# First and second mixture: tokens listed by expert, 39 gathered tiles of 128 in place of eight dense experts

## The reference, cut to what matters

```python
x = x + tanh(g_xattn[0]) * attention0(ctx, layernorm(x))
# layer 0: xf = layernorm(x), 2048 x 128
spk = (xf @ Wg.T + bg > 1.0)                     # 2048 x 8
topv, topi = top_k(spk, 2);  topw = softmax(topv)
for e in range(8):
    h = silu(xf @ w1[e].T + b1[e]) * (xf @ w3[e].T + b3[e])   # 512 wide
    y = (h > 1.0) @ w2[e].T + b2[e]
    out += comb[:, e] * y                        # comb: topw at topi, zero elsewhere
x = x + tanh(g_ffn[0]) * out
# layer 1: attention, then a ternary feed-forward part (silu, gelu, gelu)
# layer 2: attention, then
idx, scores = top_k(xf @ Wg + bg, 2) with softmax
h = gelu(xf @ W1[e] + b1[e]);  y = h @ W2[e] + b2[e]
out = layernorm(xf + sum over the two of score * y) * gamma + beta
x = x + tanh(g_ffn[2]) * out
# layer 3: attention, then a mixture of eight small experts (not touched)
```

## Time and profile before

| | us |
|---|---|
| median of three runs | 1279.51 |
| lowest, highest | 1269.94, 1280.77 |
| profiled execution, whole | 1281.16 |
| its span (first to last instruction) | 1279.8 |

### The profile page before, as it was taken

The page is one execution under the profiler, slowest core; times in us unless marked ns, Lnnn a source line. Parts: engine busy times, 40 slices in busy tenths (PEclk is TensorE's granted clock), DMA queues, the critical chain, the costliest instruction groups (busy, mean ns, idle before and its releaser), DMA issues.

```text
span 1279.8 us, 22233 instructions
## 1 busy us (share of the span) xinstructions
PE 1075.3 (84%) x8405; PEld 822.7 (64%) x8405; DVE 795.9 (62%) x1613; ACT 514.1 (40%) x846; POOL 314.7 (25%) x545
## 2 busy tenths in 40 slices
PE   3677799999999679997777899899954888888888
PEld 2455677777777556766566677677742667767655
DVE  3677568788887863333245367999983456652555
ACT  0344544333333223322134377667720245554412
POOL 5233111232221222224334012332234112200200
PEclk9978999999999589998589789999985599996999
DMA  4300001321210200000100012313000000000162
GB/s 145 115 11 11 7 26 30 100 74 63 92 33 1 91 0 1 1 1 34 54 20 23 10 34 68 92 50 91 34 0 9 18 15 15 16 16 2 38 207 94
DMA packets 35176, 55.70 MB, mean 44 GB/s; under 512 B 4192, under 2 KB 18048, under 8 KB 34816
## 3 DMA queue, kind: packets, MB, share of 16 engines
q1 hardware_dynamic: 34640, 53.11, 13.7%
q10 hardware_dynamic: 432, 1.18, 0.2%
HBM read 47.26 MB, written 1.25 MB: 38 GB/s over the span
## 4 chain that ended last, share of the span: by engine, by line
PE 59%; DVE 20%; issue 6%; ACT 5%; DMA 4%; POOL 4%; SPq 1%; POOLq 0%; DVEq 0%; ACTq 0%
PE banks L386 9%; PE banks L159 8%; PE banks L161 8%; PE banks L160 8%; DVE NM L456 4%; PE banks L394 4%; PE bank L407 4%; PE bank L1604 2%; PE bank L1407 2%; PE bank L159 2%; DMA QT<-NMT 2%; DVE TT L1391 2%; PE bank L161 2%; PE bank L160 2%; ACT EE L430 2%
## 5 line engine op out<-in xcount | busy, mean ns | idle before, releaser
L456 DVE TENSOR_REDUCE NM<-banks 128x4 f32<-128x1024 f32 (+1 forms) x112 | 136.9, 1222 | 159.8 <-PE banks L386 159.8
L386 PE MATMUL banks<-KT,QT 31*128 31x128 f32 (+1 forms) x1280 | 163.1, 391 | 73.7 <-DMA QT<-NMT 25.1
L386 PEld LDWEIGHTS banks<-KT,QT 31*128 31x128 f32 x1280 | 114.9, 227 | 107.0 <-issue 37.0
L430 ACT ACTIVATE EE<-banks 128x1024 f32<-128x1024 f32 x112 | 114.6, 1024 | 166.9 <-PE banks L394 166.8
L394 PE MATMUL banks<-QT,KT 32*128 32x128 f32 x1792 | 155.9, 317 | 4.7 <-ACT EE L430 3.5
L1384 ACT ACTIVATE SG<-banks,VC 128x512 f32<-128x512 f32 x128 | 88.2, 689 | 151.0 <-PE banks L161 150.9
L394 PEld LDWEIGHTS banks<-QT,KT 32*128 32x128 f32 x1792 | 129.0, 214 | 8.9 <-issue 6.6
L1391 DVE SCALAR_TENSOR_TENSOR TT<-banks,VC,SG 128x512 f32<-128x512 f32 x128 | 95.9, 749 | 48.8 <-ACT SG L1384 45.8
L1444 ACT ACTIVATE DEP<-banks,VC 128x512 f32<-128x512 f32 x128 | 87.8, 688 | 63.1 <-PE banks L161 60.8
L1301 POOL TENSOR_TENSOR ACC<-ACC,TM 128x512 f32<-128x512 f32 x48 | 65.2, 1360 | 181.4 <-DVE TM L1287 180.8
L1461 DVE TENSOR_TENSOR HP<-DEP,HP 128x512 fp32r<-128x512 f32 x128 | 95.9, 768 | 17.7 <-ACT HP L1449 15.0
(11 more groups left out here) (261 smaller groups left out, 2285.3 us busy)
## 6 DMA issues: line engine op xcount, KB each, us to landing
CBS<-cw SPq DMA_DIRECT2D x96, 256.0 KB, 4.8
RAW<-in_w SPq DMA_DIRECT2D x8, 768.0 KB, 4.7
RAW<-in_w SPq DMA_DIRECT2D x8, 512.0 KB, 4.2
RAW<-in_w SPq DMA_DIRECT2D x4, 704.0 KB, 4.9
KT<-KQ SPq DMA_DIRECT2D x32, 64.0 KB, 1.9
QT<-KQ SPq DMA_DIRECT2D x32, 64.0 KB, 1.9
CTX<-in_ctx SPq DMA_DIRECT2D x3, 512.0 KB, 4.7
X<-in_x SPq DMA_DIRECT2D x4, 256.0 KB, 4.4
```

The lines of the kernel that those rows point to most:

```text
L386: ins = pe.matmul(out, self.QT[r, b1 % 4, 128 * g:128 * g + 128], moving(r, 128 * g), start=True, stop=True)
L430: act.activation(self.EE[:, b % 2, 2 * p:2 * p + 2, :].rearrange("p i k -> p (i k)"), self.K.SB[:, :], ACT.Exp).then_inc(sig("ee").sem, 1)
L456: dve.tensor_reduce(out, src, AX.X, ALU.max, negate=True).then_inc(sig("m1").sem, 1)
```

## The change

Three classes are new: `Router` (with `Router0`, `Router2`) takes the place of `Early` in Attn0 and Attn2; `Routed` (with `Routed0`, `Routed2`) takes the place of `Summed`, `Experts0` and `Experts2`.

**Router, beside the attention.** Its methods are called once per stage `s` by each engine's loop, and for six more stages behind the last one. Group `g` begins at stage 4g + 3 + behind (behind is 4 in Attn0, whose last stage is 19, and 5 in Attn2, whose last is 20), and goes through phases one stage apart: 0 statistics (DVE) and reciprocal root (POOL); 1 normalized tokens on ACT, and SyncE waits for them and stores the four batches to DRAM (`xn`); 2 transpose and copy; 3 four logit products, the largest (9 DVE operations), a power on POOL; 4 the second largest, weights, running counts (14); 5 two products that rank the tokens of each expert, and places (7); 6 eight indirect DMAs by POOL that write token numbers into `list` in DRAM, 4 bytes for each of 128 tokens. Beside it 16 weight chunks of 128x512 are split (ACT high, POOL low) at stages 2 to 17, fed by eight transfers of 512 KB.

```diff
+class Router:
...
+    def sp(self, s):
...
+        if s == 0:
+            sp.wait_ge(*sig("r_zero")(1))
+            sp.dma_start(self.list.rearrange("(c p) o -> c (p o)", p=128), self.XT[:, 0:128]).then_inc(sig("list_zero").sem, 16)
+        n = (s - 1) // 2
+        if s >= 1 and s % 2 == 1 and n < self.chunks // 2:
+            self.sp_weights(n)
+        g = self.phase(s, 1)
+        if g is not None:
+            sp.wait_ge(*sig("xn")(g + 1))
+            for i in range(4):
+                b = 4 * g + i
+                sp.dma_start(self.xn[128 * b:128 * b + 128, :], self.XNB[:, g % self.homes, 128 * i:128 * i + 128]).then_inc(sig("xn_out").sem, 16)
...
+    def pool(self, s):
...
+        if s == 0:
+            self.pool_init()
...
+        if 2 <= s < 2 + self.chunks:
+            self.lo(pool, s - 2)
+        g = self.phase(s, 3)
+        if g is not None:
+            pool.wait_ge(*sig("w_diff")(g + 1))
+            pool.tensor_tensor(self.RM[:, 4, :], K.EXPB[:, 0:4], self.RM[:, 3, :], ALU.pow).then_inc(sig("w_pow").sem, 1)
+        g = self.phase(s, 6)
+        if g is not None:
+            pool.wait_ge(*sig("pos")(g + 1))
...
+            for i in range(4):
+                for j in range(2):
+                    b = 4 * g + i
+                    pool.indirect_dma_start(self.list, bass.IndirectOffsetOnAxis(ap=self.PI[:, j, b:b + 1], axis=0),
+                                            self.TOK[:, b:b + 1], None).then_inc(sig("listed").sem, 16)
```

**Routed, the mixture.** First a table: from the counts of the eight experts, which of them own which of 39 tiles of 128 tokens (six small products with DVE operations between), the expert number of each tile as an integer, and the token numbers, once SyncE has read `list` back. Then tile by tile, tokens stationary and weights moving, at an address that a register gives:

```diff
+class Routed:
...
+    def pool_gather(self, t):
...
+        if t >= 4:
+            pool.wait_ge(*sig("xt_done")(t - 3))
+        pool.indirect_dma_start(self.XG[:, t % 4, :], None, self.R.xn,
+                                bass.IndirectOffsetOnAxis(ap=self.IDX[:, t:t + 1], axis=0)).then_inc(sig(f"xg{t % 4}").sem, 16)
...
+    def expert(self, t):
...
+        return pe.value_load(self.ETU[0:1, t:t + 1], min_val=0, max_val=7)
+    def of(self, W, v, a, b):
+        return W[:, bass.DynSlice(v, 1), a:b].rearrange("p o k -> p (o k)")
+    def pe_product(self, t, v, bank, a, n, bias):
+        pe = self.K.nc.tensor
+        xh, xl, one = self.XH[:, t % 2, :], self.XL[:, t % 2, :], self.ONE[:, t % 4, :]
+        wh, wl = self.of(self.R.WH, v, a, a + n), self.of(self.R.WL, v, a, a + n)
+        pe.matmul(bank, xh, wh, start=True, stop=False)
+        pe.matmul(bank, xh, wl, start=False, stop=False)
+        pe.matmul(bank, xl, wh, start=False, stop=False)
+        return pe.matmul(bank, one, self.BI[:, bias:bias + n], start=False, stop=True)
     def pe(self):
...
+        self.pe_table()
+        self.pe_turn(0)
+        es = {}
+        for i in range(self.NT + 2):
+            if i + 1 < self.NT:
+                self.pe_turn(i + 1)
...
+                pe.wait_ge(*sig("xl")(i + 1))
+                pe.wait_ge(*sig("one")(i + 1))
+                es[i] = self.expert(i)
+                self.pe_first(i, es[i])
+            if 0 <= i - 1 < self.NT:
+                self.pe_units(i - 1)
+            if 0 <= i - 2:
+                self.pe_second(i - 2, es[i - 2])
+    def dve_result(self, t):
...
+        dve.wait_ge(*sig("second")(t + 1))
...
+        dve.tensor_copy(self.Y[:, t % 3, :], self.ybank(t)[:, 0:128]).then_inc(*K.dv.up())
+        dve.wait_ge(*K.dv.now())
+        dve.tensor_tensor(self.Y[:, t % 3, :], self.ybank(t)[:, 128:256], self.Y[:, t % 3, :], ALU.add).then_inc(sig("y").sem, 1)
+    def pool_sums(self, b):
...
+        if b == 0:
+            pool.wait_ge(*sig("y_pos")(1))
+            for t in range(self.NT - 3, self.NT):
+                pool.wait_ge(*self.stored(t))
+        if b >= 4:
+            pool.wait_ge(*sig("summed")(b - 3))
+        for j in range(2):
+            pool.indirect_dma_start(self.GA[:, b % 4, j, :], None, self.ys,
+                                    bass.IndirectOffsetOnAxis(ap=self.R.PI[:, j, b:b + 1], axis=0)).then_inc(sig(f"ga{b % 4}").sem, 16)
...
+class Routed0(Routed):
...
     def pool(self):
...
+        for c in range(E8):
+            hi, lo, src = self.second_weights(c)
+            pool.wait_ge(*sig("w2_hi")(c + 1))
+            pool.tensor_tensor(lo, src, hi.bitcast(F32), ALU.subtract).then_inc(sig("w2_lo").sem, 1)
+        super().pool()
...
+    def pe_second(self, t, v):
...
+        if t == 0:
+            pe.wait_ge(*sig("w2_lo")(8))
+        if t >= 1:
+            pe.wait_ge(*sig("y")(t))
+        pe.wait_ge(*sig("st")(t + 1))
+        for k in range(4):
+            pe.matmul(y, self.ST[:, t % 2, 128 * k:128 * k + 128],
+                      self.W2[:, bass.DynSlice(v, 1), k, :].rearrange("p o d -> p (o d)"), start=(k == 0), stop=False)
+        pe.matmul(y, self.ONE[:, t % 4, :], self.BI[:, 1024:1280], start=False, stop=True).then_inc(sig("second").sem, 1)
```

```diff
+        K.features(st, "1")
-        for k in range(4):
-            K.raw_freed[raw0 + k] = K.sig("w1_lo")(4 * (k + 1))
+        for k in range(self.PIECES):
+            K.raw_freed[raw0 + k] = K.sig("w1_lo")(2 * (k + 1))
```

More of the change, by code:

```diff
@@ L30 @@
 CP_COLS = [("ident", 128), ("tri", 128), ("dec", 128), ("iota", 128), ("ones", 128), ("iop", 1),
-           ("kx", 1), ("qx", 1)]
+           ("kx", 1), ("qx", 1), ("before", 128), ("ecol", 64), ("first", 8), ("i128", 1), ("i32", 1)]
 def places(cols):
@@ L76, with done @@
 class Names:
+    OWN = ["listed"] + [f"{n}{i}" for n in ("xg", "ga") for i in range(4)]
     def __init__(self, nc, ctx):
         self.nc, self.ctx = nc, ctx
-        self.made = {}
+        self.made, self.free = {}, []
     def __call__(self, name):
         if name not in self.made:
-            self.made[name] = Sig(self.nc, self.ctx, name)
+            own = name in self.OWN or not self.free
+            self.made[name] = Sig(self.nc, self.ctx, name) if own else self.free.pop()
         return self.made[name]
+    def done(self, name, n):
+        s = self(name)
+        s.base += n
+        if name not in self.OWN:
+            self.free.append(self.made.pop(name))
 def heads4(ap):
@@ L127, in sb, with features @@
         return stack.enter_context(self.nc.sbuf_tensor(name, shape, dt))
+    def features(self, stack, tag):
+        self.XTh, self.XTl = (self.sb(stack, f"XT{n}{tag}", [128, 2048], F32R) for n in "hl")
     def cp(self, n):
@@ new lines, with weights, chunk, sp_weights @@
+class Router0(Router):
+    homes = 1
+    def weights(self, st):
+        K = self.K
+        self.WH, self.WL = (K.sb(st, f"W13{n}", [128, E8, 1024], F32R) for n in "HL")
+    def chunk(self, c):
+        e, a = c // 2, 512 * (c % 2)
+        return self.WH[:, e, a:a + 512], self.WL[:, e, a:a + 512], self.K.raw(self.raw0 + e)[:, a:a + 512]
+    def sp_weights(self, n):
+        self.K.sp_raw(self.raw0 + n, self.K.A["w0"][:, n, 0:1024], 1024)
+class Router2(Router):
+    homes = 4
+    def weights(self, st):
+        K = self.K
+        self.WH, self.WL = (K.sb(st, f"W12{n}", [128, E8, 512], F32R) for n in "HL")
+        self.W2 = K.sb(st, "W22", [128, E8, 4, 256], F32R)
+    def chunk(self, c):
+        e, src = c % 8, self.K.raw(self.raw0 + c // 2)[:, 512 * (c % 2):512 * (c % 2) + 512]
+        if c < 8:
+            return self.WH[:, e, :], self.WL[:, e, :], src
+        return self.W2[:, e, :, 0:128], self.W2[:, e, :, 128:256], src.rearrange("p (k d) -> p k d", k=4)
+    def sp_weights(self, n):
+        half, e = n // 4, 2 * (n % 4)
+        self.K.sp_raw(self.raw0 + n, self.K.A["w2"][:, e:e + 2, 512 * half:512 * half + 512], 1024)
@@ L1499, in dve_finish2, with pool_sums @@
                                      op0=ALU.mult, op1=ALU.add)
+    def pool_sums(self, b):
+        super().pool_sums(b)
+        if b % 4 == 2 and b > 4:
+            self.K.pool_rsqrt(b // 4, b // 4 - 1, 4)
+        if b == NBAT - 1:
+            self.K.pool_rsqrt(NGRP, NGRP - 1, 4)
 class Experts3(Experts):
@@ L2114, in counts @@
                                   "u_turned": n, "ft": n, "ut": n, "kq": n, "kqc": n, "proj": n, "outp": n,
-                                  "x_done": n} | {f"keys_in{i}": 16 * 4 for i in range(4)}
+                                  "x_done": n} | {f"keys_in{i}": 16 * 4 for i in range(4)} | {f"kx{i}": 1 for i in range(5)} | {f"context_in{i}": 16 for i in range(4)}
     def sp(self):
         K, H, sig, sp = self.K, self.H, self.K.sig, self.K.nc.sync
+        self.sp_keys(0)
         for s in range(0, self.LAST + 1):
@@ L2300, in programs, with first_two @@
     P.dve()
-def attention_and_experts(K, attention, experts, tag, raw0, src, WN, parts, behind, bank):
+def first_two(K):
     with ExitStack() as both:
-        early = Early(K, both, tag, raw0, src, WN, parts, behind, bank)
+        router = Router0(K, both, "0", 0, "Wg0", "bg0", True, 4, 4, 6, 16)
         with ExitStack() as st:
-            P = attention(K, st, early)
+            P = Attn0(K, st, router)
             programs(P)
@@ L2310, in attention_and_experts, with third_two, last_two @@
         with ExitStack() as st:
-            P = experts(K, st, early)
```

(34 more changed lines are left out.)

914 lines of the change are left out of this document (620 added, 294 removed).

## The result

The changed kernel takes 1481.18 us (median of four runs, 1465.12 to 1482.08) against 1277.74 us of the kernel before: a ratio of 1.158, interval 1.152 to 1.165. It is slower, on the side that was forecast, but by 203 us where 26 were forecast, and outside the range. Runs of one kernel differ: those of the kernel before on record go from 1262.8 to 1281.2. The profiled execution has a span of 1480.2 us.

The account below looks back on a forecast made before the run. TensorE was taken to bound the mixtures, and waits in chains the attentions. First layer -20, third +40, Mlp +5, Attn3 +1: +26 in total, 1307 us profiled, 1306 median; likeliest 1292 to 1345, full range 1240 to 1390.

Parts of the forecast that it names:

- c: GpSimd's cost of one indirect DMA, taken as 1.2 us (0.6 to 2.9); 49 on the path a layer, 98 in all.
- 24 scatters (hidden while GpSimd is 35% busy): Both attentions: scatters ahead of the tail add nothing; part of +4 us each for small operations, scatters and weight halves.
- scatters that delay the values: Named sign of being wrong: GpSimd's scatters delaying the values in the attentions would add to their +18 and +21 us.
- The first mixture's tile: TensorE's products and transposes 3.0 us plus 0.3 for the expert's register load and addresses: 3.3 us, 39 tiles 129 us.
- rival B: Register load and address arithmetic stand on TensorE's queue each tile, 1.9 us: +80 us, total 1386; chance 0.17.
- The third layer's tile: Chain through TensorE, ACT and DVE, second product waiting for the previous tile's `y`: 3.77 us, taken as 4.0; tiles 156 us.
- SyncE's wait: Both attentions: SyncE waits for `xn` and issues four stores before the queries; +9 us in the first, +13.5 in the third layer.
- First attention, the rest: First attention: +4 us for DVE's and GpSimd's small operations, 24 scatters, and 16 ACT and 16 GpSimd weight halves.
- Startup, Mlp, last attention: Startup before the tiles 23 us in the first layer, 7 in the third; Mlp +5 us; last attention +1 us.
- A (cheap descriptors): Rival: an indirect DMA costs GpSimd only 0.6 us, making the change faster, 1247 us; chance 0.28.
- C: Rival: gains and costs cancel over the whole kernel, total 1267 to 1292 us; chance 0.17.
- D: Rival: GpSimd is held up while DVE's adds read two SBUF operands beside the summing gathers: +22 us, 1328; chance 0.05.

## Why the prediction was wrong

- **Price of an indirect DMA.** Right: 1.25 against 1.2, and its places too: sums 40 and 46 us (forecast 41 each), tails 29.3 and 30.1 (26). The range for c, 0.6 to 2.9, was the widest term of the sum and hid that the errors lay elsewhere: by c alone the result would have wanted 3.0.
- **"24 scatters (hidden while GpSimd is 35% busy)".** This step failed, and it is the largest error. I counted the issue on GpSimd and not what the writes do to others' transfers and to the drain, which the sum has at nothing. The sign of being wrong that I named, scatters that delay the values, went by GpSimd's time too. Closely packed, they delay landings and the drains of the stage: 69 us between the changed kernel and the one with spread writes, of which the traces put 13 and 34 in the two attentions and 11 and 12 in the drains.
- **The first mixture's tile.** 4.09 us against 3.3. I counted the bias products as any other product; two of 64 rows and 512 columns and one of 256 columns cost 1.0 us a tile. With 128 rows the tile took 3.1, the forecast's sum for TensorE alone being 3.0. The 0.3 for the register, and rival B, were wrong: with a fixed address the tile stays at 4.08, and the third layer's goes from 4.08 to 4.00.
- **The third layer's tile.** 4.08 against 4.0. The chain was right (3.77 forecast, 3.79 without the 64-row product), the rest was luck: I added 0.23 for a falling clock, which stayed at 0.97 over these tiles, and the 64-row product that I had not seen put in 0.29.
- **SyncE's wait.** Right in place and cause, 14 and 17 forecast, 18 and 23 measured. What the forecast left out is the clock after a stall; that this is the whole of the difference is argued and not measured.
- **First attention, the rest.** +4 forecast for small operations; 25 remain when scatters and SyncE's wait are gone. This term failed too, and its cause is open; added work on DVE lengthens this attention, which makes DVE's operations a likely part.
- **Startup, Mlp, last attention.** Right (23.6, 4.8, 1), but for the third layer's startup, 15 against 7, where the load of the biases comes first on SyncE's queue (3.3 us in the chain) and the table waits for it.
- **Rivals.** A (cheap descriptors) is refuted by c. C and D did not happen; DVE's adds beside the summing gathers did not slow them: their pitch is 1.25, that of the scatters, which have no such adds beside them, 1.26.

## What to carry to other kernels

A transfer costs its issuer's time and what it does to the landings of others: before a scatter of single words into a packed table is called hidden, ask what else uses the queues then, and try the words 64 bytes apart, which was enough here. Products of fewer rows between full ones are not free fillers; here padding them with zeros took 1.0 us off a tile of 4.1. And in a stage held by chains, a wait can cost more than its length: look at the granted clock right behind it, which was half here.

## What the runs showed of the hardware that was not expected

- 4-byte indirect writes packed closely: the stage's drain behind them takes 10.6 to 21 us, with 64 bytes between entries 2.7; a 64 KB load issued among them was followed by 24 us of waiting, and a 512 KB load landed in 13.8 us instead of 4.2. Their semaphore updates go on for 8 to 18 us behind their last packet, and stop within half a microsecond when the entries are apart.
- A 64-row product between 128-row ones: 0.76 us for it and its successor together, where two full ones take 0.46; its weight load starts only with it.
- An indirect DMA of 128 rows costs GpSimd 0.95 us and 0.30 between two, the same for rows of 4, 64 and 512 bytes.
